# A decoder layer on one core: the first expert product computed transposed, one copy moved to ScalarE, a second PSUM bank

## The reference

```
x = x + attention(layernorm(x))           # linear attention, four 512x512 projections
x = x + experts(layernorm(x), token_ids)
x = x + ternary_ffn(layernorm(x))         # 512 -> 2048 -> 512, weights -1, 0, 1 times a scale

# the middle step, with one expert to each token, chosen by its id:
g = silu(h @ ctx[e].T); u = h @ ctx[e].T  # both use the same weights
out = (g * u) @ ctx[e].T                  # and so does the third product
```

## Time and profile before

| | us |
|---|---|
| median of 3 runs | 768.12 (767.45 to 768.91) |
| profiled execution, first to last instruction | 762.1 |
| TensorE matmul busy | 718.1 (94%) |
| TensorE weight loads busy (beside matmuls) | 380.7 (50%) |
| VectorE busy | 388.6 (51%) |
| ScalarE busy | 276.1 (36%) |
| GpSimd busy | 108.5 (14%) |

### The profile page before, as it was taken

One profiled execution on the slowest core, in us unless ns is written; L12 is line 12 of the kernel. 1 busy time (PEld: TensorE's weight loads), 2 busy tenths in 40 slices (PEclk: granted clock), 3 DMA queues, 4 the chain that ended last, 5 costly groups with the idle time before them and its releaser, 6 DMA issues.

```text
span 762.1 us, 11832 instructions
## 1 busy us (share of the span) xinstructions
PE 718.1 (94%) x3882; PEld 380.7 (50%) x3883; DVE 388.6 (51%) x672; ACT 276.1 (36%) x430; POOL 108.5 (14%) x154
## 2 busy tenths in 40 slices
PE   4999999999996789999994999999999999999997
PEld 2465556566464556555553444444444444444443
DVE  5568666676537855444457343453434434343223
ACT  3465554555454355222224222222222222222221
POOL 4203034033021400000005000000000000000000
PEclk9999999999998999999997999999999999999999
DMA  7983034033044396222212000020000100010001
GB/s 223 391 320 143 1 127 151 0 129 147 1 173 159 130 342 232 78 91 83 83 42 70 27 15 14 14 71 14 15 0 14 69 14 14 0 55 1 0 0 55
DMA packets 32493, 66.73 MB, mean 88 GB/s; under 512 B 6352, under 2 KB 6352, under 8 KB 31440
## 3 DMA queue, kind: packets, MB, share of 16 engines
q1 hardware_dynamic: 28464, 53.24, 20.1%
q0 software_dynamic: 4000, 13.11, 5.0%
HBM read 47.73 MB, written 18.61 MB: 87 GB/s over the span
## 4 chain that ended last, share of the span: by engine, by line
PE 85%; DVE 5%; DMA 3%; issue 2%; ACT 2%; POOL 2%; SPq 1%; DVEq 0%; POOLq 0%; ACTq 0%
PE bank L1056 31%; PE bank L1314 29%; PE bank L1324 14%; PE bank L1049 6%; PE bank L1199 2%; PE bank L1213 1%; DMA nrm<-in_L_ffn_W_down_dram 1%; PE bank L1234 1%; DMA stage<-in_L_attn_Wv_dram 1%; DVE w_att L843 1%; DVE w_att L842 1%; SPq L183 1%; POOL rs L305 1%; DVE st L568 1%; DMA n<-sorted_outputs,pos_now 0%
## 5 line engine op out<-in xcount | busy, mean ns | idle before, releaser
L1314 PE MATMUL bank<-w_att,region 128*128 128x512 f16 (+1 forms) x1024 | 233.1, 381 | 0.8 <-ACT w_att L535 0.8
L1314 PEld LDWEIGHTS bank<-w_att,region 128*128 (+1 forms) x1024 | 100.5, 98 | 120.5 <-issue 3.6
L1022 DVE SCALAR_TENSOR_TENSOR tmp<-tmp,hk,bank 128x512 f32<-128x512 f32 x64 | 47.8, 747 | 153.7 <-PE bank L1314 153.3
L1324 PE MATMUL bank<-region,tmpA 128*128 (+1 forms) x504 | 119.1, 379 | 0.0
L1056 PE MATMUL bank<-w_moe,tmpA 128*128 x456 | 104.6, 379 | 1.5 <-DVE tmpA L913 1.5
L1056 PE MATMUL bank<-xT,w_att 128*128 128x512 f16 x384 | 88.6, 387 | 4.3 <-DVE region L753 2.3
L543 ACT ACTIVATE tmp<-bank,qs 128x512 f32<-128x512 f32 x64 | 44.0, 688 | 125.1 <-PE bank L1314 125.1
L547 ACT ACTIVATE tmpA<-tmp 128x512 f16<-128x512 f32 x64 | 40.4, 631 | 121.7 <-DVE tmp L1022 121.7
L1324 PEld LDWEIGHTS bank<-region,tmpA 128*128 128x128 f16 x504 | 49.2, 98 | 59.6 <-DVE stage L1005 0.9
L1056 PEld LDWEIGHTS bank<-w_moe,tmpA 128*128 128x128 f16 x456 | 44.4, 98 | 47.1 <-issue 1.7
L1025 DVE TENSOR_TENSOR tmpA<-tmp,tmpA 128x512 f16<-128x512 f32 x64 | 44.3, 692 | 45.7 <-ACT tmpA L547 45.7
(11 more groups left out here) (134 smaller groups left out, 752.4 us busy)
## 6 DMA issues: line engine op xcount, KB each, us to landing
stage<-in_L_ffn_W_up_dram SPq DMA_DIRECT2D x8, 1024.0 KB
stage<-in_L_ffn_W_gate_dram SPq DMA_DIRECT2D x8, 1024.0 KB, 7.0
sorted_tokens<-a SPq DMA_DIRECT2D x10, 512.0 KB, 10.3
n<-sorted_tokens SPq DMA_DIRECT2D x20, 256.0 KB, 2.6
stage<-in_ctx_dram SPq DMA_DIRECT2D x4, 1024.0 KB
stage<-in_L_ffn_W_down_dram SPq DMA_DIRECT2D x4, 1024.0 KB
nrm<-in_L_ffn_W_down_dram SPq DMA_DIRECT2D x4, 1024.0 KB, 7.4
out_dram<-stage SPq DMA_DIRECT2D x16, 256.0 KB, 2.1
```

The costliest lines, as they stand in the source:

```text
L1022: dve.scalar_tensor_tensor(out=h32, in0=sil, scalar=hk[:, 0:1], in1=gate_ps[:, :], op0=ALU.mult, op1=ALU.mult).then_inc(s["hid_mul"], 1)
L1314: mm = pe.matmul(dst, w[:, bass.ds(cf_c, 1), k * P:(k + 1) * P].rearrange("p a n -> p (a n)"), x3T[:, bass.ds(b, 1), i, k].rearrange("p a ...
L1324: mm = pe.matmul(ffy_ps[t][:, :], hid[:, parity, i, t * P:(t + 1) * P], tern[2][:, bass.ds(c, 1)].rearrange("p a n -> p (a n)"), start=(st ...
```

## The change

- z is computed transposed. The stationary operand is a 128 x 128 block of w_moe, the moving one a 128-column slice of xsT: 48 matmuls of 128 columns in place of 12 of 512. h32 then has the hidden features on the partitions, as the second product needs it, and its four transposes and bank th_ps are gone; hT's high half is copied from h32 by ScalarE, its low half computed from h32 by VectorE.
- The bank of th_ps becomes a second bank for z; tile n uses bank n % 2.
- The second product does its eight matmuls with hT's high half first (waiting for that alone), then the four with the low half.
- y is copied out by ScalarE, behind the high half of the next tile's hT.
- Two banks by three slots make a loop body of six tiles, run twice, behind tiles 0 to 6 written out.

```diff
-    z_ps, y_ps, tx_ps, th_ps, q_ps = ps[0], ps[1], ps[2], ps[3], ps[4:8]
+    z_ps, y_ps, tx_ps, q_ps = (ps[0], ps[3]), ps[1], ps[2], ps[4:8]
...
 # ScalarE
+        def y_copy(i, slot, uses):
+            act.wait_ge(s["y_mm"], i + 1)
+            act.wait_ge(s[f"ys_out{slot}"], 16 * uses)
+            act.activation(ys_slot[slot], y_ps[:, :], ACT.Copy, scale=CTX_SCALE ** -2).then_inc(s["y_evac"], 1)
+
-        def tile_step(i, units=()):
+        def tile_step(i, bank, units, prev_slot, prev_uses):
             act.wait_ge(s["z_mm"], i + 1)
             act.wait_ge(s["h_mul"], i)
-            act.activation(sil, z_ps[:, :], ACT.Silu, scale=1.0 / CTX_SCALE).then_inc(s["z_act"], 1)
+            act.activation(sil, z_ps[bank][:, :], ACT.Silu, scale=1.0 / CTX_SCALE).then_inc(s["z_act"], 1)
             xs_hi(i + 1)
             for g, j in units:
                 unit_copies(g, j)
-            act.wait_ge(s["th_mm"], i + 1)
+            act.wait_ge(s["h_mul"], i + 1)
             act.wait_ge(s["y_mm"], i)
-            act.activation(hT[:, 0], th_ps[:, :], ACT.Copy).then_inc(s["h_hi"], 1)
+            act.activation(hT[:, 0], h32, ACT.Copy).then_inc(s["h_hi"], 1)
+            if prev_slot is not None:
+                y_copy(i - 1, prev_slot, prev_uses)
...
 # VectorE
-        def tile_step(i, quant, prev_slot, prev_uses):
+        def tile_step(i, bank, quant):
             if quant is not None:
                 signs_of(*quant)
             dve.wait_ge(s["z_act"], i + 1)
-            dve.wait_ge(s["h_hi"], i)
-            dve.tensor_tensor(h32, z_ps[:, :], sil, ALU.mult).then_inc(s["h_mul"], 1)
+            dve.wait_ge(s["h_lo"], i)
+            dve.tensor_tensor(h32, z_ps[bank][:, :], sil, ALU.mult).then_inc(s["h_mul"], 1)
             xs_lo(i + 1)
-            if prev_slot is not None:
-                y_copy(i - 1, prev_slot, prev_uses)
             dve.wait_ge(s["h_hi"], i + 1)
-            dve.tensor_tensor(hT[:, 1], th_ps[:, :], hT[:, 0], ALU.subtract).then_inc(s["h_lo"], 1)
+            dve.tensor_tensor(hT[:, 1], h32, hT[:, 0], ALU.subtract).then_inc(s["h_lo"], 1)
...
 # TensorE
-            moe(z_ps[:, :], xsT, e).then_inc(s["z_mm"], 1)
+        def first(i, bank):
+            e = expert(i)
+            pe.wait_ge(s["xs_lo"], i + 1)
+            if not (isinstance(i, int) and i < 2):
+                pe.wait_ge(s["h_mul"], i - 1)
+            for r in range(T):
+                steps = [(p, j, k) for k in range(K) for p, j in PARTS]
+                for n, (p, j, k) in enumerate(steps):
+                    mm = pe.matmul(z_ps[bank][:, r * P:(r + 1) * P],
+                                   w_moe[:, bass.ds(e, 1), j, k, r * P:(r + 1) * P].rearrange("p a d -> p (a d)"),
+                                   xsT[:, p, k * P:(k + 1) * P], start=(n == 0), stop=(n == len(steps) - 1))
+            mm.then_inc(s["z_mm"], 1)
+
+        def second(i):
+            e = expert(i)
+            pe.wait_ge(s["y_evac"], i)
+            pe.wait_ge(s["h_hi"], i + 1)
+            for k in range(K):
+                for j in range(2):
+                    pe.matmul(y_ps[:, :], hT[:, 0, k * P:(k + 1) * P], w_of(e, j, k), start=(k == 0 and j == 0), stop=False)
+            pe.wait_ge(s["h_lo"], i + 1)
+            for k in range(K):
+                mm = pe.matmul(y_ps[:, :], hT[:, 1, k * P:(k + 1) * P], w_of(e, 0, k), start=False, stop=(k == K - 1))
+            mm.then_inc(s["y_mm"], 1)
+
+        def tile_step(i, bank, units, slot, slot_count, begins):
+            first(i, bank)
             xs_transpose(i + 1, slot, slot_count)
-            if not first:
+            if not begins:
                 second(i - 1)
             for g, j in units:
                 unit_transposes(g, j)
-            pe.wait_ge(s["h_mul"], i + 1)
-            pe.wait_ge(s["h_lo"], i)
-            transposes(th_ps, lambda k: h32[:, k * P:(k + 1) * P]).then_inc(s["th_mm"], 1)
...
-        with pe.Fori(1, 6) as g:
-            for j in range(3):
-                tile_step(3 * g + j + 1, (), (j + 2) % 3, g + 1 + (j + 2) // 3, False)
+        for n in range(1, 7):
+            tile_step(n, n % 2, ((2, n - 1),) if n <= 3 else (), (n + 1) % 3, 1 + (n + 1) // 3, False)
+        with pe.Fori(1, 3) as g:
+            for n in range(1, 7):
+                tile_step(6 * g + n, n % 2, (), (n + 1) % 3, 2 * g + 1 + (n + 1) // 3, False)
```

## The result

The changed kernel takes 785.51 us (785.02 to 787.55) beside 768.28 us for the kernel before; the ratio is 1.0254, with an interval of 1.0228 to 1.028. A second comparison, with both kernels run beside each other again, gave 1.0233 (1.0209 to 1.0256). The direction and the mechanism forecast were right; the rise was 17.2 us on the timed runs and 21.3 us between the two profiled spans, where 25.0 had been forecast.

A forecast was written before the change was run, and what follows sets the result against it. TensorE bounds the kernel, and the first product becomes limited by its sequencer's address steps: 18.8 + 5.6 + 1.1 - 0.5 = +25.0 us takes the span from 762.1 to 787.1, plus 6.0 gives 793.1 us; range 784 to 804.

The forecast's parts named there:

- tile 1's z: Expert stage, tile 1: addresses begin at 279.3 as before, z ends at 283.6 instead of 282.5, +1.1 us.
- tiles 2 to 4: Tiles following a step with a unit: the full queue holds the sequencer, 3 x 1.85 = +5.6 us against 7.85 a tile.
- tiles 5 to 18: Fourteen plain tiles of the expert stage: 7.4 us for 6.06 each, 14 x 1.34 = +18.8 us.
- tail of the expert stage: Last y product: y's end comes 7.25 us after z's instead of 7.7; with the shorter copy -0.5 us.
- rest: No change outside 270 to 400 us; y_copy on ScalarE and two z banks each priced at 0.
- The price of an address step: TensorE's sequencer: 0.13 us for each address, matmuls included; 32 addresses in the first product, 31 intervals, 4.03 us.
- the fixed parts of the round: Sequencer's ways between a tile's two products, 1.2 us each, in a round of 7.34 rounded up to 7.4 us.
- From span to time: Whole kernel: runs lie 6.0 us above the profiled span, so a span of 787.1 becomes 793.1 us.
- A: Rival, first product: address steps stay hidden and TensorE's work decides, 5.72 us a tile for 6.06, 761.5 us; chance 0.07.
- B: Rival, first product: dearer address steps, intervals of 0.15 to 0.16 us, 0.4 us more a tile, 800 us; chance 0.10.
- C: Rival, first product: array slower on narrow matmuls, 98 ns weight loads not hidden, 7.73 us a tile, 798 us; chance 0.05.
- D: Rival, expert stage: TensorE's granted clock falls; at 1.2 GHz +4 us a tile, some 860 us in all; chance 0.02.

The follow-up runs named there:

- the narrow variant of before: The kernel before with only z's moving operand taken in four blocks of 128 columns, not transposed: 790.0 us beside 765.3 for the kernel before.
- the first experiment: The changed kernel with the first product always taking expert 0, so its 32 address steps a tile are gone: 757.3 us beside 765.3 for the kernel before.

## Why the prediction was right, and by how much it was off

By its own steps, from profile to profile (before's Silu of tile 4 and 18 at 306.1 and 390.8, see above):

| step | forecast | measured |
|---|---|---|
| tile 1's z | +1.1 | +0.3 |
| tiles 2 to 4 | +5.6 | +5.2 |
| tiles 5 to 18 | +18.8 | +15.6 |
| tail of the expert stage | -0.5 | 0.0 |
| rest | 0 | +0.2 |
| span | +25.0 | +21.3 |

*The price of an address step* was right: 31 intervals of 0.13 us were to be 4.03 us, and the row above has 350.2 to 354.3; the stage's nineteen products run from 4.0 to 4.2, and the mean of all their intervals is 0.131 us. That it is a price of the sequencer, for each different slice with a run-time address, is shown by the experiments with 0, 16, 24 and 32 such addresses (tiles of 5.71, 5.71, 6.16, 7.16 us; the first two are set by TensorE's own work) and by the narrow variant of before.

*The largest error is in tiles 5 to 18, in the fixed parts of the round.* Each way between the two products was put at 1.2 us. Measured are 1.0 and 1.1 in the tile above, and 1.1 and 1.1 on average of the fourteen, the turns of the loop (1.4 and 1.6) included. The way read from before (304.1 to 305.3) had two more register computations in it than most of the new tiles have, ahead of the load of 304.5 in the earlier trace rows:

```profile
L1257 PEldq FUSED_REGOPS  x1: 42/42/42, 304.2 to 304.2; - x1
L1262 PEldq FUSED_REGOPS  x2: 37/94/151, 304.4 to 304.9; - x2
```

(The first row, and the first of the two in the second.) Besides, I rounded up three times. The round was put at 7.40 and is 7.16: 0.24 us a tile, which over fourteen tiles is the difference.

*Tile 1.* The matmuls of z took as long as forecast (278.7 to 282.8), but the unit in front of it began 0.55 us earlier than in before's profile. That start hangs on weights landing; it varied by 1.6 us between two profiles of the same kernel. In the second pair of profiles, Silu of tile 1 comes 3.2 us earlier in the changed kernel than in the one before (282.9 and 286.1). So one pair of profiles can neither confirm nor refute a term of 1.1 us here; whether the change moves this start is open.

*Tiles 2 to 4.* The queue's room was read correctly. In the changed kernel the unit begins at 286.2 and the sequencer comes to the next load at 287.0, again 0.8 us later: 15 of the unit's 32 matmuls had begun, and 17 were still queued. It is 17 behind each unit of tiles 1 to 3, in both kernels (timeline, then line 1262):

```profile
286.20 1.95 PE L1234 MATMUL bank<-ident_b,w_att 128*128 128x128 bf16 x32
```

```profile
L1262 PEldq TENSOR_LOAD <-tile_expert x1: 295/295/295, 287.0 to 287.0; - x1
```

The 64 instructions given by the Trainium skill ("TensorE: Matmul & The Clock Gate", Architectural detail) would have let it come there as the unit began; the trace disagrees a second time.

*The tail* failed at a wait I had priced at nothing. I wrote that the next y product comes 3 us after ScalarE's copy. It does in every tile but the last, where it follows at once: y of tile 18 waited for the copy of y of tile 17 behind hT's high half (the 1.35 us above). It ate the half microsecond that the missing transposes gave.

*From span to time.* I added 6.0 us because the runs stood that much above the profiled span. In every execution where both are known the time is 1.6 us above its own span (785.03 and 783.4, 767.5 and 765.9). So the first profile of before belongs to an execution of some 763.7 us, 4.6 below the median, and the changed kernel's to one 0.5 below. That is the 4.1 us between the two differences, 21.3 and 17.2. The forecast of 793.1 is 7.6 us too high: 3.7 by the sum (25.0 for 21.3), 4.1 by the profile it was added to. That the measured time still lies within the range, at its low end, it owes in part to the width of the range. With 1.6 in place of 6.0 my sum would have given 788.7.

*The rivals.* A (steps stay hidden) is what the first experiment makes: 8.0 us faster than before, forecast 6.6. That it would decide below 22 addresses fits with 24 being slower by 0.1 us a tile and 16 being faster by 0.34. B (dearer steps) didn't occur: the interval is 0.124 us with one narrow matmul behind a step or two. C is out by 2.68 us for 48 matmuls, and with it the 81 ns of the Trainium skill (same page, Back-to-back issue gap): the trace has 0.056 us a pair with free addresses and 0.076 to 0.085 with an address for every one and a half, which comes near that figure, for a reason of its own. D: the granted clock is 1.00 in this stretch too (columns as in the earlier trace rows):

```profile
306.00:416.00 110.00, 105.00 (x986) 72.66 (x982) 29.85 (x45) 36.32 (x65) 8.11 (x15) 1.00 0.21 70
```

Still open: within a product most address steps follow each other by 0.124 us, but every eighth by 0.15 to 0.28. In the changed kernel it is every eighth without exception, that is once in 32 instructions (8 steps, 12 weight loads, 12 matmuls). What the longer ones wait for no run here shows. They make up the difference between 3.84 and 4.1 us.

## What to carry to other kernels

Before cutting a matmul with a run-time address in narrower pieces, count the different slices: each costs the sequencer about 0.13 us, and as soon as this is more than the matmuls behind it take, the engine is limited by its feeding, though its busy share stays at 94% and hardly a wait is shown. Look for it in the first and last start of the address steps, not in the engine's idle time; and buy the addresses off (a copy to a fixed place, made ahead on a queue with time to spare) rather than the arithmetic in them. Add a change to the time of the profiled execution itself, and ask how usual that execution is.

## What the runs showed of the hardware that I had not expected

- An address step costs its interval, not its duration: 46 ns of work come every 0.124 us, and a plain addition of 32 ns still every 0.11 us.
- One or two matmuls and their weight loads behind a step make no difference to the 0.124 us, 512 or 128 columns wide, and the register may address either operand.
- The load of one number to a register of TensorE, 0.30 us in most tiles, took 1.15 and 1.05 us while the DMA engines were 80% and 86% busy, beside the copies of the low half; in the changed kernel it took 0.58 and 0.56 us at 85% and 79%. That the transfers are the cause is likely, but no run tests it.
